# Spectral tower of a token network on one core: the product over channels in four 64x64 matmuls, edge counts by pairs of bins, and the sorting work spread anew

## The chip, the cores and the metric

The kernel runs on one core of a Trainium2 chip. The number that counts is the device time of one execution, in microseconds (us). A core has five engines: TensorE (PE, with its weight loads shown apart as PEld), VectorE (DVE), ScalarE (ACT), GpSimd (POOL) and SyncE (SP), which issues most of the DMAs. Engines wait for each other on semaphores.

## The reference

The reference is a chain of stages on 128 images of 64x64 values (for the later stages 8192 tokens of 64 values). The first stage, a Fourier tower, is what the change touches:

```python
def fourier_layer(x, fw_i):                      # x: batch, 32 channels, 64, 64
    x_ft = jnp.fft.rfft2(x, s=(M, N), norm='ortho')
    lo = jnp.einsum('bixy,ioxy->boxy', x_ft[:, :, :M1, :M2], w_lo)    # M1 = M2 = 12
    hi = jnp.einsum('bixy,ioxy->boxy', x_ft[:, :, -M1:, :M2], w_hi)
    ...
    return jnp.fft.irfft2(out_ft, s=(M, N), norm='ortho')

h = conv1x1(concat([x, grid]), p_w, p_b)         # 3 -> 32 channels
for i in range(4):
    x1 = fourier_layer(h, fw[i])
    x1 = relu(conv1x1(x1, w1_w[i], w1_b[i]))
    x1 = conv1x1(x1, w2_w[i], w2_b[i])
    h = h + x1
h = relu(conv1x1(h, q1_w, q1_b))                 # 32 -> 4 channels: the head
h = conv1x1(h, q2_w, q2_b)                       # 4 -> 1
```

Then come attention and expert layers (named a0, e0, a1, e1, a2, e2, a3), and at the end a graph attention over 262,144 edges and 8192 self loops. The kernel needs the edges sorted by their target node. It sorts them in two passes of a counting sort, and hides that work beside the stages before: DVE ranks, POOL scatters.

## The kernel before, in words

**The tower's loops.** 128 images go in 4 groups of 32. Each group passes 4 layers; a group and a layer are a unit (16 units, `u`). A unit has 4 chunks of 8 images (`ch`), so there are 64 chunks, numbered n = 4u + ch here. Chunk 0 of a unit also holds what the unit does once: `mix` (L568, spectral weights), `turn` (L579) and, in all but the last layer, `blend` (L673) at the end of the unit before. A first layer also has a prologue (L519 to L547).

**A chunk on PE.** `to_x` (L597) transforms along x: 128 matmuls of 96 rows by 32 columns. Then the 32 channels come in 8 steps `s` of 4 channels: `to_y` (L638) transforms two steps at a time into four PSUM banks (banks 0 to 3), ACT applies bias and relu into the buffer `rr` (L752), and `use` (L600) reads it twice. The first reader, L615, is the product over channels: it collects, for the head, what this layer adds to the 4 head channels. It is a 128x128 weight `proj` with 512 columns, once for each half `hf` of the 64 y values, accumulated over the 8 steps in banks 4 and 5. The partitions of `rr` are (4 channels, 32 y), so `proj` is 4x4 numbers, each times a 32x32 identity. The second reader, L624, transforms back along y with 96 columns (8 matmuls per step, full 128x128 weights). The last layer of a group doesn't need it. `from_x` (L659) ends a chunk in the other layers. All this is fp32; PE runs each fp32 matmul as two instructions.

**What ties a chunk to DVE.** After the 8 steps DVE adds banks 4 and 5 to `qa` (L847, two instructions) and signals `q_added`. The first L615 of the next chunk waits for it, since it overwrites bank 4. DVE does its share of the sorting of this chunk before that add (`rank_part(n)`, L832). So a chunk ends when both are through, PE with its steps and DVE with its sorting items and the add.

**The sorting items.** First pass (columns): 128 bins are counted over 2112 keys per partition (`count`, L2600, one bin per instruction), 52 of them by ACT ahead of the tower; PE sums the counts once (L611, L612, before the first L615 of chunk `column_offset_at`, which waits for the counts, and then for DVE's offsets, L2612 to L2616); then 6 parts of the keys (132, 176, 264, 484, 528 and 528 wide) are ranked, one item for each bin: a compare, a running sum, a copy of one column and a predicated copy (L2619, L2622, L2625, L2626). When a part is ranked, POOL scatters it: one indirect DMA for each of the 2112 columns (L2661). Second pass (rows): when POOL is through, SP loads the scattered pairs (L455), DVE makes keys (L2656, L2657), counts 65 bins and ranks 4 parts of 528, 260 items in all. Items that the tower has no room for come in fixed places later: 8 at the tower's end, TOKEN_ITEMS in the stage that loads the tower's output and all weights (`token_stage`, L3377), 16 in a0, 90 in e0.

**What sets the order.** `slot_us(n)` gives each chunk a time budget in us, `spread_items` fills it with items at planned costs (2.5 for a count, 0.4 + 0.0042 x width for a rank), and `column_plan` and `row_plan` hold the item numbers at which each chunk starts. The row pass may begin at chunk ROW_CHUNK = 51. SP loads the scattered pairs when its program comes to that chunk and POOL has signalled `scattered`.

Of the kernel before, what the change touches and what calls it, by code (L numbers as in the profile page):

```python
# [14 lines left out]
P = 128  # L15
NB = 128
S = 64
D = 64
# [93 lines left out]
def fno_constants():  # L112
# [26 lines left out]
    s2 = s2[0:2, :, :, :, :, 0:2].reshape(24, 2, 2 * 64).transpose(1, 0, 2)  # L139
    gap = np.zeros((8, 2 * 64))  # L140
    c["to_y"] = np.concatenate([s2[0], gap, s2[1], gap] * 2, 0)
    c["from_y"] = f1.reshape(P, 2 * 96)
# [19 lines left out]
    c["eye32"] = np.tile(np.eye(32), (4, 1))  # L162
# [8 lines left out]
def fno_layout(x, p_w, p_b, fw, w1_w, w1_b, w2_w, w2_b, q1_w, q1_b, q2_w, q2_b):  # L171
# [26 lines left out]
    b1 = np.zeros((LAYERS, 4, 32, 8), f32)  # L198
    w2r = np.zeros((LAYERS, CH, 8, 4, 32), f32)
    for cg in range(8):  # L200
        for cc in range(4):
            b1[:, cc, :, cg] = w1_b[:, channel(cg, cc), None]
            w2r[:, :, cg, cc] = w2_w[:, :, channel(cg, cc), None]
# [5 lines left out]
    o["q1_rep"] = np.repeat(q1_w.T[:, :, None], 32, 2).reshape(CH, P)  # L209
    o["q1_b_rep"] = np.repeat(q1_b, 32)[:, None]  # L210
    o["q2_rep"] = np.repeat(q2_w[0], 32)[:, None]
# [7 lines left out]
def fno_prelude(t, d, f, ranks):  # L219
# [6 lines left out]
    with ExitStack() as ctx:  # L226
# [6 lines left out]
        proj = sb("proj", [P, LAYERS, 8, 4, 32])  # L233
# [4 lines left out]
        with t.stage("even_in", "odd_in", "small_in", "fold_done", "fold_turned", "s_done", "s_moved", "b_sum", "qb_done", "own", "even_kept", "odd_kept", "proj_kept", "proj_ready", "fold_crossed", "under_counted") as \  # L238
# [51 lines left out]
            def _(v):  # L290
                c = Chain(v, own)
                early = iter(range(ACT_BINS, EARLY_COUNTS))

                def count_some(n):
                    for i in itertools.islice(early, n):
                        ranks.count(v, c, i, COLS)

                count_some(5)
# [3 lines left out]
                c.link(v.tensor_scalar(f.head[:], const["eye32"][:], q2_rep[:, 0:1], None, ALU.mult))  # L302
                count_some(5)
                v.wait_ge(s_done, 1)
                c.link(v.tensor_copy(proj_s[:].rearrange("p l c o -> p (l c o)")[:, 0:32 * LAYERS + 4], t.bank[7][:, 0:32 * LAYERS + 4]))
                eye = const["eye32"][:].unsqueeze(1).broadcast_to([P, 4, 32])
                for l in range(LAYERS):
                    for j in range(8):
                        c.link(v.tensor_tensor(proj[:, l, j], eye, bc(proj_s[:, l, j, :], 32), ALU.mult))
                c.link(v.tensor_tensor(f.proj0[:].rearrange("p (o y) -> p o y", y=32), eye, bc(proj_s[:, LAYERS, 0, :], 32), ALU.mult))  # L310
                v.sem_inc(proj_ready, 1)
                v.wait_ge(qb_done, 1)
                c.link(v.tensor_tensor(f.qb[:], t.bank[6][:, 0:1], q1_b_rep[:], ALU.add))
                for l in range(LAYERS):
# [8 lines left out]
                    if l in (1, 2):  # L323
                        count_some(8 if l == 1 else EARLY_COUNTS - ACT_BINS - 18)

# [21 lines left out]
class Fno:  # L347

    def __init__(self, t, ctx, d):
        sb = lambda name, shape: t.sb("f_" + name, shape, ctx=ctx)  # L350
        self.const = {k: sb(k, d[k].shape) for k in ("to_x", "to_y", "from_y", "from_y1", "from_x", "eye32", "lift", "q2_b_rep")}
# [3 lines left out]
        self.head = sb("head", [P, 32])  # L355
# [3116 lines left out]
```

## Time and profile before

| | us |
|---|---|
| three timed runs | 10031.47, 10034.33, 10067.39 |
| median | 10034.33 |
| span of the profiled execution | 10048.4 |
| TensorE busy in it | 8145.5 (81%) |
| VectorE busy | 7005.4 (70%) |
| ScalarE busy | 4663.9 (46%) |
| GpSimd busy | 5541.9 (55%) |

The profiled execution has no other time than its span of 10048.4 us, which lies between the timed runs. The tower with its preparation takes the first 4033 us of it. The page shows busy shares; for a stretch the table by windows is of more use, since each stage has another limit. Times in a timeline are the start from the span's beginning, then the duration. Matmuls overlap, so the distance between two starts tells more than a duration. "x4" is the number of instructions merged into a row.

### The profile page before, as it was taken

The page shows a single profiled execution, that of the slowest core. Times are in us where ns is not written, and L with a number is a line of the kernel's source. Part 1 is how long each engine was busy: PE and PEld are TensorE (multiplying, and loading weights), DVE is VectorE, ACT ScalarE, POOL GpSimd, SP SyncE. Part 2 cuts the span into 40 slices and gives each one's busy share as a digit, 9 for nine tenths or more (in the row PEclk, how much of TensorE's full clock was granted, in tenths as well). Part 3 has the DMA queues.
Part 4 walks back from the last instruction along what each step waited for, and adds up shares of the span by engine and source line. Part 5 has one row for each costly group of instructions (what it writes and reads, how often), then busy time and mean ns, then how long its engine had stood idle before and what let it go on. Part 6 is the DMA issues. An engine that isn't in the chain of part 4 may idle for free. (4 is left out here: it accounts for less than half of the span.)

```text
span 10048.4 us, 187067 instructions
## 1 busy us (share of the span) xinstructions
PE 8145.5 (81%) x76884; PEld 4885.9 (49%) x76884; DVE 7005.4 (70%) x10524; ACT 4663.9 (46%) x10721; POOL 5541.9 (55%) x5545
## 2 busy tenths in 40 slices
PE   4899899999999998477788888887767688888837
PEld 2666566656666665222222222223332577777732
DVE  7898888740000677678999999995454578888852
ACT  5333444444444434233677877784333333333322
POOL 0077777777777000174566666676243077777740
PEclk7999899989998999588899999997667589999966
DMA  5000100010001000100000000000100022222210
GB/s 182 22 24 25 58 27 25 26 38 23 23 23 37 31 24 4 35 2 1 3 2 2 2 2 2 2 2 1 1 1 1 13 44 45 51 45 45 46 51 9
DMA packets 275177, 251.33 MB, mean 25 GB/s; under 512 B 204433, under 2 KB 258449, under 8 KB 268628
## 3 DMA queue, kind: packets, MB, share of 16 engines
q1 hardware_dynamic: 97012, 219.26, 6.7%
q0 software_dynamic: 177312, 20.11, 3.4%
q8 instruction: 607, 9.95, 0.4%
q14 instruction: 246, 2.02, 0.1%
HBM read 178.16 MB, written 60.82 MB: 24 GB/s over the span
## 5 line engine op out<-in xcount | busy, mean ns | idle before, releaser
L2507 POOL DMA_INDIRECT sorted<-by_row_rows,r_pos x2112 | 2086.7, 988 | 2170.6 <-ACT e_xt L1354 1096.2
L2661 POOL DMA_INDIRECT sorted<-r_rows,r_pos x2112 | 2142.8, 1015 | 1153.2 <-issue 642.7
L2180 DVE TENSOR_TENSOR a_top<-bank,a_k 128x2048 f32<-128x2048 f32 x896 | 1972.5, 2278 | 8.5 <-ACT a_qs L2235 6.9
L2960 PE MATMUL bank<-g_parts,g_hot 128*128 128x256 bf16 x11088 | 1326.2, 286 | 250.0 <-issue 136.1
L2943 POOL DMA_INDIRECT g_g<-table,g_el x1188 | 1169.9, 985 | 362.3 <-issue 362.3
L2960 PEld LDWEIGHTS bank<-g_parts,g_hot 128*128 128x128 bf16 x11088 | 1133.0, 103 | 443.0 <-issue 144.1
L2382 PE MATMUL bank<-a_top,sc_pick_row 128*32 128x512 f32 x7168 | 953.2, 616 | 307.0 <-DVE a_top L2180 291.4
L2622 DVE TENSOR_TENSOR_SCAN r_work<-r_hit,r_base 128x528 f32<-128x528 bf16 (+4 forms) x1028 | 1072.8, 1044 | 33.6
L615 PE MATMUL bank<-f_space,f_proj 128*128 128x512 f32 x2048 | 988.3, 610 | 90.7 <-ACT f_space L752 82.5
L847 DVE TENSOR_TENSOR f_qa<-f_qa,bank 128x512 f32<-128x512 f32 x128 | 82.2, 684 | 1354.5 <-PE bank L624 1141.1
L2228 ACT ACTIVATE a_over<-a_k,a_qs 128x64 f32<-128x64 f32 x4096 | 1021.4, 337 | 0.0
L752 ACT ACTIVATE f_space<-bank,f_b1r 128x512 f32<-128x512 f32 x1024 | 635.2, 686 | 451.9 <-PE bank L638 451.9
L624 PEld LDWEIGHTS bank<-f_from_y,f_space 128*128 128x128 f32 x6144 | 748.5, 192 | 185.1 <-issue 185.1
L624 PE MATMUL bank<-f_from_y,f_space 128*128 128x96 f32 x6144 | 739.3, 274 | 0.0
L615 PEld LDWEIGHTS bank<-f_space,f_proj 128*128 128x128 f32 x2048 | 354.2, 190 | 578.4 <-issue 426.5
L2626 DVE COPY_PREDICATED r_work<-r_hit,r_work 128x528 f32<-128x528 uint16 (+4 forms) x1028 | 613.7, 597 | 0.0
L743 ACT ACTIVATE f_space<-bank 128x384 f32<-128x384 f32 x384 | 188.6, 491 | 900.7 <-PE bank L624 900.7
L2382 PEld LDWEIGHTS bank<-a_top,sc_pick_row 128*32 128x32 f32 x7168 | 151.5, 109 | 878.0 <-DVE a_top L2180 757.4
L1423 DVE TENSOR_TENSOR e_hid<-e_hid,bank 128x512 f32<-128x512 f32 x512 | 345.8, 686 | 310.5 <-ACT e_hid L1382 172.7
L2972 ACT ACTIVATE g_apart<-g_near,sc_place 128x512 f16<-128x512 f16 x462 | 307.7, 713 | 509.5 <-DMA g_near<-near 311.9
L597 PE MATMUL bank<-f_to_x,f_bb 96*32 96x128 f32 x16384 | 499.8, 284 | 31.9 <-ACT f_bb L732 31.9
L638 PE MATMUL bank<-f_space,f_to_y 56*64 56x512 f32 x4096 | 498.5, 602 | 20.4 <-ACT f_space L737 20.4
(587 smaller groups left out, 11825.1 us busy)
## 6 DMA issues: line engine op xcount, KB each, us to landing
f_wm<-folded SPq DMA_DIRECT2D x16, 4608.0 KB
sorted<-r_rows,r_pos POOLq DMA_INDIRECT x2112
sorted<-by_row_rows,r_pos POOLq DMA_INDIRECT x2112, 2.1
g_near<-near SPq DMA_DIRECT2D x231, 128.0 KB
states<-g_st SPq DMA_DIRECT2D x33, 768.0 KB, 4.0
g_g<-table,g_el POOLq DMA_INDIRECT x1188
fp_raw<-t_modes SPq DMA_DIRECT2D x4, 2304.0 KB, 15.4
folded<-fp_turned SPq DMA_DIRECT2D x16, 576.0 KB, 9.3
```

The costliest lines, as they stand in the source:

```text
L615: last = pe.matmul(t.bank[4 + hf][:, :], proj[:, cg].rearrange("p o y -> p (o y)"), rr[:, s % 3 * 2 + hf, :], start=(s == 0), stop=(s == 7))
L624: last = pe.matmul(t.bank[6 + s % 2][:, b * 96:(b + 1) * 96], rr[:, s % 3 * 2 + hf, b * P:(b + 1) * P], const["from_y"][:, hf * 96:(hf + 1 ...
L752: last = act.activation(rr[:, s % 3 * 2 + hf, :], t.bank[s % 2 * 2 + hf][:, :], ACT.Relu, bias=f.b1r[:, u % LAYERS, cg:cg + 1])
L2180: v.tensor_tensor(top[:, n % RD].rearrange("p q (h s) -> p q h s", s=S), q, kk, ALU.max).then_inc(top_done, 1)
L2228: last = act.activation(over[:, slot, q, e, :], ks[:, k % 2, e, :], ACT.Relu, scale=-1.0, bias=qs[:, k % 2, slot, at_q:at_q + 1])
L2382: last = pe.matmul(sums[k % 2][32 * q:32 * q + 32, :], t.pick_row[:, i, :], rhs, start=False, stop=(i == I16 - 1), skip_group_check=True)
L2507: p.indirect_dma_start(out=self.dst, out_offset=bass.IndirectOffsetOnAxis(ap=self.idx[:, k:k + 1], axis=0), in_=self.rows[:, k, :], in_off ...
L2622: c.link(v.tensor_tensor_scan(self.run[:, 0:n], self.hit[:, 0:n], self.hit[:, 0:n], self.base[:, i:i + 1], ALU.add, ALU.bypass))
L2626: c.link(v.copy_predicated(self.posf[:, 0:n], self.hit[:, 0:n].bitcast(mybir.dt.uint16), self.run[:, 0:n]))
L2661: p.indirect_dma_start(out=self.dst, out_offset=bass.IndirectOffsetOnAxis(ap=self.pos[:, at:at + 1], axis=0), in_=self.rows[:, part % 2, a ...
L2943: p.indirect_dma_start(out=g[:, c % GB, j, :], out_offset=None, in_=d["table"], in_offset=bass.IndirectOffsetOnAxis(ap=el[:, at, 0:1], axi ...
L2960: last = pe.matmul(out, hot[:, n % HB, k, j * P:(j + 1) * P], parts[:, k, s].rearrange("p f i -> p (f i)"), start=(k == 0 and s == 0), sto ...
```

## The change

Four things change together.

**1. The product over channels.** y is now split in sixteens: the partitions of `rr` are (2 halves of 16 y, 4 channels, 16 y). The product then doesn't mix the upper and the lower 64 partitions, and each 128x128 matmul becomes two of 64 rows by 64 columns. For the second `hf` the output halves are swapped (`part ^ hf`), so that the four matmuls of a step stand in the four different quadrants of the array.

**2. The transform to y.** To write its output in that order, each 56x64 matmul of `to_y` becomes two of 56x32: 16 matmuls where 8 stood, in 8 different places (2 of 64 rows, 4 of 32 columns).

**3. The counts.** `count_two` counts two bins in one instruction: a key of the upper half of the bins is folded onto the lower half and weighs 4096, others weigh 1; the sum is split into two counts afterwards. 76 column counts become 38 instructions, 65 row counts 33, with three preparing instructions and five splitting ones for each pass.

**4. The plan.** The budgets, the first row chunk, and with them all item numbers change. The preparation holds 26 pair counts where it held 21 counts. The offsets come in chunk 0, not 1. A chunk without a unit's extra work from number 17 to 27 still has 16 ranks; such a chunk of a last layer has 8 where it had 10. The tower now holds 86 row ranks, not 137, and TOKEN_ITEMS, which takes what is left, is 60, not 9.

The core of the diff:

```diff
@@ to_y and use
                     for hf in range(2):
-                        last = pe.matmul(t.bank[4 + hf][:, :], proj[:, cg].rearrange("p o y -> p (o y)"), rr[:, s % 3 * 2 + hf, :], start=(s == 0), stop=(s == 7))
+                        for part in range(2):
+                            rows, to = slice(64 * part, 64 * part + 64), 64 * (part ^ hf)
+                            last = pe.matmul(t.bank[4 + hf][to:to + 64, :], proj[rows, cg].rearrange("p o y -> p (o y)"), rr[rows, s % 3 * 2 + hf, :], start=(s == 0), stop=(s == 7), skip_group_check=True)
...
                                 base = half_of(cg, k)
-                                last = pe.matmul(t.bank[s % 2 * 2 + hf][64 * k:64 * k + 64, :], const["to_y"][base:base + 56, hf * 64:(hf + 1) * 64], aa[base:base + 56, cg, :], start=True, stop=True, skip_group_check=True)
+                                for part in range(2):
+                                    to, col = 64 * part + 32 * k, 64 * hf + 32 * part
+                                    last = pe.matmul(t.bank[s % 2 * 2 + hf][to:to + 32, :], const["to_y"][base:base + 56, col:col + 32], aa[base:base + 56, cg, :], start=True, stop=True, skip_group_check=True)
@@ the counts
-    def count(self, v, c, i, n):
-        c.link(v.tensor_scalar(self.seen[:, 0:n], self.key[:, 0:n], self.t.iota[:, i:i + 1], None, ALU.is_equal, ALU.add, accum_out=self.hist[:, i:i + 1]))
+    def pair_bins(self, v, c, first, pairs):
+        c.link(v.tensor_scalar(self.seen, self.key[:], float(first + pairs), None, ALU.is_ge))
+        c.link(v.tensor_scalar(self.weight, self.seen, SECOND - 1.0, 1.0, ALU.mult, ALU.add))
+        c.link(v.scalar_tensor_tensor(self.low_key, self.seen, -float(pairs), self.key[:], ALU.mult, ALU.add))
+
+    def count_two(self, v, c, first, j):
+        c.link(v.scalar_tensor_tensor(self.seen, self.low_key, float(first + j), self.weight, ALU.is_equal, ALU.mult, accum_out=self.two[:, j:j + 1]))
+
+    def part_bins(self, v, c, first, pairs):
...
@@ the plan
-EARLY_COUNTS = 73
-ROW_CHUNK = 51
+EARLY_PAIRS = 26
+ROW_CHUNK = 54
...
     if ch:
-        return 28 if u % LAYERS == LAYERS - 1 else 44
+        return 23 if u % LAYERS == LAYERS - 1 else 42
     if u % LAYERS == 0:
-        return 131 if u else 143
-    return 53 if u % LAYERS == LAYERS - 1 else 67
+        return 126 if u else 110
+    return 47 if u % LAYERS == LAYERS - 1 else 61
...
-            if done == offset and spent > 18:
+            if done == offset and spent > (40 if n == 0 else 18):
```

The order of instructions on PE, from the last transform of the first unit through its first chunk's first two steps, before. Names are output<-inputs; `f_space` is the buffer that holds `aa` and `rr`, `f_proj` is `proj`, and the sizes are columns of the weight by columns streamed:

```order
L597 MATMUL bank<-f_to_x,f_bb 32x128 x128
L638 MATMUL bank<-f_space,f_to_y 64x512 x8
L615 MATMUL bank<-f_space,f_proj 128x512 x2
L624 MATMUL bank<-f_from_y,f_space 128x96 x8
L638 MATMUL bank<-f_space,f_to_y 64x512 x8
L615 MATMUL bank<-f_space,f_proj 128x512 x2
```

The same place after the change:

```order
L606 MATMUL bank<-f_to_x,f_bb 32x128 x128
L651 MATMUL bank<-f_space,f_to_y 32x512 x16
L620 MATMUL bank<-r_hist,sc_before 128x128
L621 MATMUL bank<-r_hist,sc_ones 128x128
L626 MATMUL bank<-f_space,f_proj 64x512 x4
L635 MATMUL bank<-f_from_y,f_space 128x96 x8
```

The transform to y has twice the matmuls at half the width, the product twice the matmuls at half the width and half the rows, and the two sums over the counts now stand in the first chunk.

DVE, from the end of the preparation to the first rank of the tower, before. `x3` and `x55` are counts of one bin each (`r_work,r_hist<-r_key`), `f_qa` is the add that ends a chunk:

```order
L2600 TENSOR_SCALAR r_work,r_hist<-r_key,sc_iota 128x2112 x3
L321 STREAM_TRANSPOSE fp_turned<-bank 128x64 x72
L64 UNCONDITIONAL_BRANCH
L790 UNCONDITIONAL_BRANCH
L2600 TENSOR_SCALAR r_work,r_hist<-r_key,sc_iota 128x2112 x55
L2607 SCALAR_TENSOR_TENSOR r_hist<-r_under 128x52
L2608 TENSOR_TENSOR r_hist<-r_hist,r_under 128x52
L847 TENSOR_TENSOR f_qa<-f_qa,bank 128x512 x2
L2612 SCALAR_TENSOR_TENSOR r_base<-bank,r_hist 128x128
L2615 TENSOR_TENSOR r_base<-r_base,bank 128x128
L2616 TENSOR_TENSOR r_base<-r_base,bank 128x128
L2619 TENSOR_SCALAR r_hit<-r_key,sc_iota 128x132
```

DVE at the same place after the change, without the five rows that split the sums:

```order
L2630 SCALAR_TENSOR_TENSOR r_work,r_base<-r_pos 128x2112 x7
L330 STREAM_TRANSPOSE fp_turned<-bank 128x64 x72
L64 UNCONDITIONAL_BRANCH
L803 UNCONDITIONAL_BRANCH
L2630 SCALAR_TENSOR_TENSOR r_work,r_base<-r_pos 128x2112 x12
```

```order
L2645 SCALAR_TENSOR_TENSOR r_hist<-r_under 128x52
L2646 TENSOR_TENSOR r_hist<-r_hist,r_under 128x52
L2650 SCALAR_TENSOR_TENSOR r_base<-bank,r_hist 128x128
L2653 TENSOR_TENSOR r_base<-r_base,bank 128x128
L2654 TENSOR_TENSOR r_base<-r_base,bank 128x128
L2657 TENSOR_SCALAR r_hit<-r_key,sc_iota 128x132
```

The offsets now stand ahead of the first add of the tower, with 76 ranks between them and that add, where 55 counts stood ahead of it.

## Rows read from the trace of the kernel before

**Rows 1.** The page: busy us, share of the span, instructions of PE.

```profile
PE 8145.5 (81%) x76884; PEld 4885.9 (49%) x76884; DVE 7005.4 (70%) x10524; ACT 4663.9 (46%) x10721; POOL 5541.9 (55%) x5545
```

**Rows 2.** Windows: stretch, length, busy by engine, PE clock, DMA share, GB/s.

```profile
326.40:389.40 63.00, 60.43 (x702) 44.22 (x696) 45.93 (x162) 24.41 (x45) 0.00 (x0) 0.97 0.01 2
389.40:447.00 57.60, 50.62 (x544) 35.03 (x536) 52.76 (x188) 22.61 (x41) 0.00 (x0) 0.99 0.01 2
504.00:1161.00 657.00, 600.77 (x7984) 405.78 (x7984) 576.86 (x1381) 272.75 (x504) 510.22 (x448) 0.97 0.10 32
1161.00:3490.70 2329.70, 2144.03 (x27416) 1503.10 (x27420) 979.75 (x1491) 963.93 (x1783) 1629.57 (x1662) 0.95 0.10 30
1352.40:1402.90 50.50, 49.15 (x536) 34.74 (x532) 41.08 (x68) 20.11 (x37) 38.57 (x39) 1.00 0.03 2
2302.80:2353.30 50.50, 49.15 (x540) 34.74 (x534) 1.31 (x3) 20.10 (x37) 38.31 (x41) 1.00 0.03 2
3024.80:3056.40 31.60, 28.20 (x309) 12.94 (x300) 1.28 (x2) 14.23 (x24) 24.02 (x25) 1.00 0.37 96
3490.70:4004.80 514.10, 474.03 (x6152) 315.78 (x6140) 399.21 (x621) 215.67 (x396) 0.00 (x0) 0.97 0.04 13
4033.00:4062.00 29.00, 0.00 (x0) 0.00 (x0) 22.31 (x36) 0.00 (x0) 0.00 (x0) 0.50 0.62 199
```

**Rows 3.** Timeline of PE within chunk 34: start, duration, operation, idle before.

```profile
2323.15 1.98 PE L615 MATMUL bank<-f_space,f_proj 128*128 128x512 f32 x4
2324.97 1.92 PE L624 MATMUL bank<-f_from_y,f_space 128*128 128x96 f32 x16
2326.73 1.91 PE L615 MATMUL bank<-f_space,f_proj 128*128 128x512 f32 x4
2328.47 1.92 PE L624 MATMUL bank<-f_from_y,f_space 128*128 128x96 f32 x16
2330.32 1.95 PE L638 MATMUL bank<-f_space,f_to_y 56*64 56x512 f32 x16
2332.20 0.70 PE L615 MATMUL bank<-f_space,f_proj 128*128 128x512 f32 x1
```

**Rows 4.** Timelines of PE and ACT at the start of chunk 47, last layer.

```profile
3031.55 1.95 PE L638 MATMUL bank<-f_space,f_to_y 56*64 56x512 f32 x16 [0.73 <-ACT f_space L737]
3034.85 1.98 PE L615 MATMUL bank<-f_space,f_proj 128*128 128x512 f32 x4 [1.35 <-ACT f_space L752]
...
3033.53 2.42 ACT L752 ACTIVATE f_space<-bank,f_b1r 128x512 f32<-128x512 f32 x4 [2.04 <-PE bank L638]
```

**Rows 5.** Groups of PE, 257.1 to 258.95 us: mixing of modes.

```profile
L568 PE MATMUL bank<-f_wm,f_spec 64*32 64x64 f32 x128 | 1.8, 221 | 1.6 <-issue 1.6
```

**Rows 6.** Counts, first product and offsets: by line, then timeline.

```profile
L2600 DVE TENSOR_SCALAR_CACHE_REDUCE r_work<-r_key,sc_iota x55: 2411/2412/2415, 189.3 to 321.9; 128x2112 bf16<-128x2112 bf16 x55
...
L615 PEld LDWEIGHTS bank<-f_space,f_proj x2048: 186/190/337, 287.9 to 4002.4; 128*128 128x128 f32 x187
...
339.15 0.42 DVE L2612 TENSOR_TENSOR_SCAN r_base<-bank,r_hist 128x128 f32<-128x128 f32 x1 [12.78 <-PE bank L612]
```

**Rows 7.** Groups of DVE in chunk 2, 389.4 to 447 us.

```profile
L2622 DVE TENSOR_TENSOR_SCAN r_work<-r_hit,r_base 128x132 f32<-128x132 bf16 x46 | 22.7, 493 | 1.6
```

**Rows 8.** POOL's scatter by line: ns, starts, idle; then SP's reload.

```profile
L2661 POOL DMA_INDIRECT sorted<-r_rows,r_pos x2112: 955/962/1912, 500.1 to 3295.6; - x192
...
  DVEq L810: 510.5, 2
...
3298.96 6.45 SPq L455 DMA_DIRECT2D r_rows<-sorted  x4
```

**Rows 9.** Timeline of DVE at the token stage's end and a0's start.

```profile
4051.74 1.32 DVE L2622 TENSOR_TENSOR_SCAN r_work<-r_hit,r_base 128x528 f32<-128x528 bf16 x1
...
4054.33 1.32 DVE L2622 TENSOR_TENSOR_SCAN r_work<-r_hit,r_base 128x528 f32<-128x528 bf16 x1
...
4062.14 0.69 DVE L953 TENSOR_REDUCE a_mean<-h 128x8 f32<-128x512 f32 x1 [5.65 <-PEq L72]
```

More of the change, by code:

```diff
@@ L161, in fno_constants @@
     c["grid_spectrum"] = sp.reshape(16, KYG * KX * 2 * GI)
-    c["eye32"] = np.tile(np.eye(32), (4, 1))
+    c["eye16"] = np.tile(np.eye(16), (8, 1))
+    lift_to, head_from = np.zeros((4, 32, 2, 2, 16)), np.zeros((2, 4, 16, 2, 32))
+    for hf in range(2):
+        for place in range(2):
+            for y in range(16):
+                lift_to[:, 16 * (place ^ hf) + y, hf, place, y] = 1.0
+                head_from[place, :, y, hf, 16 * (place ^ hf) + y] = 1.0
+    c["lift_to"], c["head_from"] = lift_to.reshape(P, 64), head_from.reshape(P, 64)
     return {k: np.ascontiguousarray(v.astype(np.float32)) for k, v in c.items()}
@@ L291, in _ @@
                 c = Chain(v, own)
-                early = iter(range(ACT_BINS, EARLY_COUNTS))
+                early = iter(range(EARLY_PAIRS))
                 def count_some(n):
-                    for i in itertools.islice(early, n):
-                        ranks.count(v, c, i, COLS)
-                count_some(5)
+                    for j in itertools.islice(early, n):
+                        ranks.count_two(v, c, ACT_BINS, j)
+                ranks.pair_bins(v, c, ACT_BINS, COLUMN_PAIRS)
+                count_some(4)
                 v.wait_ge(small_in, 16 * (len(small) + 5))
@@ L526, in prologue @@
                             pe.wait_ge(q0_moved, gi * 8)
[L527 removed]
+                        pe.matmul(t.bank[6 + n % 2][:, :], f.proj0[:, n // 4 * P:n // 4 * P + P], feat[:, n * 512:(n + 1) * 512], start=True, stop=True).then_inc(q0_done, 1)
                     pe.wait_ge(x0_moved, gi + 1)
@@ L680, in head @@
                             for hf in range(2):
-                                last = pe.matmul(t.bank[n][:, b * D + hf * 32:b * D + hf * 32 + 32], qa[:, hf, (8 * n + b) * P:(8 * n + b + 1) * P], f.head[:], start=True, stop=True)
+                                last = pe.matmul(t.bank[n][:, b * D + hf * 32:b * D + hf * 32 + 32], qa[:, hf, (8 * n + b) * P:(8 * n + b + 1) * P], f.head[:, hf * 32:hf * 32 + 32], start=True, stop=True)
                         last.then_inc(o_done, 1)
@@ L2589, in __init__ @@
         self.run, self.posf = work[:, 0, :], work[:, 1, :]
-        self.seen = work[:].rearrange("p a c -> p (a c)").bitcast(BF16)
+        self.seen = work[:].rearrange("p a c -> p (a c)").bitcast(BF16)[:, 0:COLS]
         self.hist = sb("hist", [P, P])
```

88 lines of the change are left out of this document (53 added, 35 removed).

## The prediction

> **What bounds the kernel now.** I read the page first: PE is busy 81% of the span [rows 1], more than any other engine, but that is a mean over stages, so the table by windows comes next [rows 2]. It shows three kinds of chunk in the tower. Chunk 34, with no sorting beside it, takes 50.5 us, of which PE is busy 49.15; chunk 18, with 16 ranks on DVE (41.08 us busy), takes the same 50.5. So an ordinary chunk (layers 0 to 2) is PE's. Chunk 47, of a last layer, takes 31.6 with PE busy 28.2. Chunks 1 and 2 take 63.0 and 57.6 us: there DVE's sorting sets the pace (46 ranks of 132 columns in chunk 2 [rows 7], DVE busy 52.76 of 57.6). The token stage, 29 us, has nothing on PE at all: DMAs (0.62 of their time) and 9 ranks on DVE. The timeline of PE then says what a chunk is made of [rows 3, 4], and the line of POOL what runs in parallel with the whole tower: the scatter from 500.1 to 3295.6 us, with the reload of its result at 3298.96, just as the row pass begins [rows 8].
>
> **The product.** A step's L615 is 4 instructions from 2326.73 to 2328.47 us, 1.74 us, 0.43 each [rows 3]. After the change 8 narrower ones stand in 4 quadrants. That quadrants run side by side is in the trace: L638 before is 16 instructions of 56x64 with 512 columns, and the next block starts 1.88 us after it, so four took 0.43 us together, as one L615 takes alone. So the product becomes 0.86 us.
>
> **The switches.** L624 takes 1.76 us ahead of L615 (2324.97 to 2326.73) but 1.85 ahead of L638; L638 takes 1.88 where four times 0.43 is 1.72; the L615 after it 1.82 instead of 1.74 [rows 3]. Going into quadrants and back out costs 0.09 + 0.16 + 0.08, about 0.34 us a pair (0.14 in, 0.2 out), from full array to full array nothing. After the change each step pays it. For the 4 steps between two L624: 1.74 becomes 0.86 + 0.34, saving 0.53. For the 4 right after a transform to y, which paid 0.2 for leaving quadrants already: 1.94 becomes 1.2, saving 0.72. Sum 4 x 0.53 + 4 x 0.72 = 5.0 us, so an ordinary chunk goes from 50.5 to 45.5. Bounds: switches between tile shapes free gives 6.9 us, twice their price gives 3.
>
> **The transform to y.** Not seen before: 64 rows by 32 columns with 512 columns streamed. Nearest is L568, 64x32 with 64 columns: 128 in 1.8 us, their starts within 1.57 us, 12.2 ns each [rows 5]. At L638's pace of 0.43 us for 512 columns, 64 columns take 54 ns, so 4.4 ran at once, above the four that every other line reaches. If eight run at once the block stays at 1.72 us; with four it becomes 3.44. I take no change, since these instructions are eight times as long, and what holds L568 at 12.2 ns can be the rate of issue; the other end is +1.72 us four times a chunk.
>
> **The last layers.** There ACT comes in. The transform starts at 3031.55, relus of its two steps at 3033.53 for 2.42 us, the product at 3034.85 [rows 4]. The next transform overwrites the banks, so it waits for both relus: 1.98 + 2.42 + 0.1 = 4.5 us a pair of steps at least. Before PE needed 5.5 (1.88 + two products + switch), so this did not bind. Four pairs, with 0.9 for the last product and 8.1 ahead of the first transform, make 27.1 us instead of 31.6: 4.5 saved, not 6.9.
>
> **DVE beside it.** 16 ranks at 2.59 us [rows 9] and the adds (1.3) make 42.9 us, under 45.5; a last-layer chunk has 8 ranks, 22.3, under 27.1. A pair count isn't in the trace; its nearest row is the single count, 2.41 us plus a read [rows 6], 2.46. I take 2.46, since both stream 2112 keys; between half and 1.1 times that the answer is the same, as in chunk 55 16 of them (39 us) lie under 45.5.
>
> **The tower's start.** The preparation gets 7 pair counts instead of 3 counts ahead of its last transposes: between 0 and 10 us later, I take 4. PE's first product, at 287.9 us [rows 6], thus comes at 292. The offsets now wait for it (2 us), and 76 ranks of 132 columns at 1.22 us (57.6 us less adds for 46 [rows 2, 7]) stand before the first add: chunk 0 ends at 388, not 326. PE waits some 50 us in chunk 1. Then, with 1.37 us for a rank of 176 columns (between 1.22 and 2.59 by width): chunk 1 has 44 ranks, to 444; chunk 2 8 + 30, to 497; chunk 3 36, to 548, where it was 504. Chunks 4 to 15: two with a unit's extra work at 85.6, six ordinary ones of which three are still DVE's (49, 47, 47), the last layer's 72 + 3 x 27.1. That is 604 us against 657 [rows 2]: chunk 15 ends at 1152, 9 us earlier than before.
>
> **The middle and the end.** Chunks 16 to 53 took 2329.7 us: 30 of them save 5.0, 8 save 4.5, together 186, so chunk 54 starts at 3296. Chunks 54 to 63 took 514.1 and save 6 x 5.0 + 4 x 4.5 = 48; the wait for the row offsets, now in an ordinary chunk with 13 ranks, takes back 3.5. The tower ends 9 + 186 + 48 - 3.5 = 239 us earlier.
>
> **POOL.** Its first part is ranked 8 ranks into chunk 2, at 455 instead of 500.1. It took 2796 us, 11 of them waiting after the first wait (510.5 less 499.7); later parts now wait for DVE about 16, 3 and 9 us. End: 455 + 2796 + 17 = 3268, reload by 3272. Chunk 54 starts at 3296, so nothing waits, with 24 us of cover; chunk 53 would have waited.
>
> **The token stage.** 51 more ranks at 2.59 (4051.74 to 4054.33 [rows 9]) are 132 us. Nothing covers them: the 29 us stage is already DVE's to its end but for 5.65 us of barrier. What the later stages do stays where it was.
>
> **Sum.** -239 + 132 = -107 us on the profiled span of 10048.4, which is 14 above the median and inside the timed runs; on the median of 10034.3 that makes 9927.
>
> **A rule against the change.** L638 before has two row groups writing one PSUM bank (k = 0 and 1 of a step) and still runs four at once [rows 3]. The Trainium skill, page "TensorEngine Tiling (Array Packing)", Restrictions and Gotchas (PSUM Pressure), says that different row tiles cannot access the same bank at the same time. By that rule the two halves of each product, which share bank 4 or 5, would run one after the other, and the trace disagrees with it, so it keeps only a small chance. The same page's Tiling Modes lists eight tiles of 64x32; no row shows eight at once.
>
> **The rivals.**
> - *Four streams, not eight.* What speaks for it: most lines stop at four, and L568 only just passes. The transform costs 6.9 us more in each ordinary chunk, so it goes to 52.4, +1.9; a last-layer chunk to 34, +2.3. Chunks 5 to 15 are then no longer DVE's but PE's: chunk 15 ends at 1228, +67; then 36 x 1.9 + 12 x 2.3 + 3.5 = 100; with the 132 of the token stage +300: 10334. It decides as soon as a block of 32 transforms takes over about 2.9 us. Chance 0.13.
> - *Halves one after the other.* A product stays at 1.72 us and pays the switches, again +1.9 in an ordinary chunk; last-layer chunks, and with them the sum, come out nearly as above: about 10300. Against it: the four at once in L638. Chance 0.03.
> - *Switches between tile shapes free.* An ordinary chunk at 43.6, hardly above DVE's 42.9. The tower then runs into POOL: chunk 54 would start at 3226, its keys wait until 3272, it ends at 3303 instead of 3342, and six more chunks save 1.9: -52 to 9877. Chance 0.14.
> - *Switches twice as dear*, or PE's clock granted low more often (it is 1.00 within chunks, 0.95 over the middle [rows 2]): +1.9 in 36 chunks, 9995. Chance 0.14.
> - The forecast itself, 9885 to 9980: 0.53. Something not seen, slower than 10090 with nothing above: 0.03.
>
> **How the numbers follow.** What a measurement of this kernel can tell from no change is about 0.5%, 50 us: 9984 to 10084. Faster: 0.53 + 0.14 + a fifth of the fourth = 0.70. Same: the rest of the fourth, 0.11. Slower: 0.19. The range runs from 9850 (free switches and a little more) to 10030 (dear switches and a preparation 10 us longer), which leaves out the two serial cases and the unseen, 0.19.
>
> **What would show it.** L626 (the product) with 8 instructions and L635 starting 1.0 to 1.1 us after it; L651, 32 instructions with the next block 1.9 us later (3.5 if four streams); chunk 34 at 45.5 us by windows; a last-layer chunk at 27; DVE's first L864 near 387; POOL's first row near 455, its last near 3267, and SP's reload before chunk 54; a token stage of 161 us. Wrong would be the whole sum if the block of transforms grows, and the size of it if switches or ACT's turn are mis-sized.

## The result and the profile after

| | us |
|---|---|
| before, four timed runs | 10031.47 to 10067.39, median 10044.83 |
| changed kernel, four timed runs | 9905.14 to 9931.88, median 9913.49 |
| ratio | 0.9866, 95% interval 0.9852 to 0.9881 |
| span of the profiled execution | 9910.4 (before 10048.4) |

The page of the changed kernel, answering to [rows 1]: busy us, share of the span, instructions.

```profile
PE 7804.4 (79%) x83028; PEld 4612.5 (47%) x83028; DVE 6834.7 (69%) x10375; ACT 4660.9 (47%) x10721; POOL 5520.2 (56%) x5545
```

PE has 6144 more instructions and is busy 341 us less. The table by windows, changed kernel, answering to [rows 2]; its stretches are chunk 0 from 292 us on (PE's first product starts at 287.6), chunk 1, chunks 4 to 15, 16 to 53, chunk 18 (with ranks), 34 (without), 47 (last layer), 54 to 63, and the token stage. A chunk ends with DVE's second add (L864).

```profile
292.00:382.00 90.00, 44.39 (x606) 29.72 (x605) 82.36 (x294) 20.08 (x36) 0.00 (x0) 0.73 0.00 1
382.00:437.10 55.10, 46.07 (x624) 31.58 (x624) 50.47 (x179) 20.07 (x36) 0.00 (x0) 0.90 0.01 2
540.40:1141.30 600.90, 538.70 (x9136) 353.22 (x9136) 526.18 (x1173) 272.53 (x504) 464.72 (x407) 0.96 0.11 34
1141.30:3290.80 2149.50, 1956.30 (x31060) 1346.15 (x31064) 822.35 (x1330) 963.00 (x1783) 1600.24 (x1638) 0.94 0.10 31
1324.20:1369.70 45.50, 44.14 (x630) 30.42 (x624) 41.01 (x67) 19.99 (x37) 34.83 (x36) 1.00 0.03 3
2195.80:2241.40 45.60, 44.24 (x636) 30.52 (x628) 1.29 (x3) 20.08 (x37) 34.62 (x37) 1.00 0.03 3
2855.80:2882.80 27.00, 22.24 (x404) 8.77 (x394) 1.28 (x2) 14.18 (x25) 20.60 (x22) 1.00 0.47 112
3290.80:3758.80 468.00, 421.50 (x7116) 271.86 (x7104) 326.79 (x473) 215.51 (x396) 0.00 (x0) 0.97 0.05 16
3785.10:3942.00 156.90, 0.00 (x0) 0.00 (x0) 149.27 (x241) 0.00 (x0) 0.00 (x0) 0.50 0.12 37
```

The tower ends at 3758.8 us instead of 4004.8, so 246 us earlier; the token stage takes 156.9 us instead of 28.9, so 128 of the 246 are lost again there. Chunks 54 to 63 took 514.1 and take 468.0; the middle took 2329.7 and takes 2149.5.

The timeline of PE within chunk 34 (start, duration, operation), answering to [rows 3]:

```profile
2213.54 1.95 PE L651 MATMUL bank<-f_space,f_to_y 56*32 56x512 f32 x32
2215.42 1.09 PE L626 MATMUL bank<-f_space,f_proj 64*64 64x512 f32 x8
2216.44 2.02 PE L635 MATMUL bank<-f_from_y,f_space 128*128 128x96 f32 x16
2218.39 1.09 PE L626 MATMUL bank<-f_space,f_proj 64*64 64x512 f32 x8
```

Read the distances between starts. The product now holds PE for 1.02 us (2215.42 to 2216.44) instead of 1.74. The 32 transforms to y hold it 1.88 us, exactly as long as the 16 before. The block behind a product, L635, has not changed at all and yet takes 1.95 us, where it took 1.76 ahead of a product and 1.85 ahead of a transform: PE now changes the shape of its tiles more often, and each change costs something (see the grouped order below).

PE and ACT at the start of chunk 47, a last layer, answering to [rows 4]:

```profile
2862.46 1.95 PE L651 MATMUL bank<-f_space,f_to_y 56*32 56x512 f32 x32 [0.73 <-ACT f_space L750]
2865.77 1.09 PE L626 MATMUL bank<-f_space,f_proj 64*64 64x512 f32 x8 [1.36 <-ACT f_space L765]
2866.92 1.95 PE L651 MATMUL bank<-f_space,f_to_y 56*32 56x512 f32 x32
```

From one transform to the next it is 4.46 us. ACT's relus of the pair:

```profile
2864.45 2.42 ACT L765 ACTIVATE f_space<-bank,f_b1r 128x512 f32<-128x512 f32 x4 [2.04 <-PE bank L651]
```

They end at 2866.87, and the next transform follows 0.05 us later: the last layers are ACT's now.

Answering to [rows 6]: the pair count (durations min, median, max), and DVE's timeline at the first offsets.

```profile
L2630 DVE SCALAR_TENSOR_TENSOR r_work<-r_pos x71: 2312/2357/2360, 46.6 to 3416.0; 128x2112 bf16<-128x2112 bf16 x71
```

```profile
286.44 0.42 DVE L2650 TENSOR_TENSOR_SCAN r_base<-bank,r_hist 128x128 f32<-128x128 f32 x1 [67.77 <-PE bank L621]
...
287.65 0.26 DVE L2657 TENSOR_SCALAR r_hit<-r_key,sc_iota 128x132 bf16<-128x132 bf16 x1
...
288.88 0.26 DVE L2657 TENSOR_SCALAR r_hit<-r_key,sc_iota 128x132 bf16<-128x132 bf16 x1
```

A pair of bins costs 2.36 us and a short read, as much as one bin did. A rank of 132 columns is 1.23 us here (287.65 to 288.88), and 76 of them stand before the add of chunk 0, which comes at 380.7.

POOL's scatter, answering to [rows 8], and SP's reload:

```profile
L2699 POOL DMA_INDIRECT sorted<-r_rows,r_pos x2112: 954/959/1914, 447.3 to 3239.6; - x192
...
  DVEq L824: 459.6, 2
```

```profile
3241.89 51.19 SPq L464 DMA_DIRECT2D r_rows<-sorted  x4
```

POOL starts its last scatter 51 us before chunk 54 starts, at 3290.8. The row of the reload spans its four DMAs, the last of which starts at 3292.8. In the token stage (answering to [rows 9]) DVE ranks without a gap until a barrier, and then comes a0's first row:

```profile
3942.00 0.69 DVE L970 TENSOR_REDUCE a_mean<-h 128x8 f32<-128x512 f32 x1 [1.22 <-PEq L72]
```

### The profile page after: what moved, and what is told of

It reads as the page before. It is cut to its first block and busy times, and to the rows that moved or that the text cites. A ratio compares the mean times of both kernels' runs of the same rounds, so it can differ in the third digit from the quotient of the medians.

```text
span 9910.4 us, 199204 instructions
## 1 busy us (share of the span) xinstructions
PE 7804.4 (79%) x83028; PEld 4612.5 (47%) x83028; DVE 6834.7 (69%) x10375; ACT 4660.9 (47%) x10721; POOL 5520.2 (56%) x5545
## 5 line engine op out<-in xcount | busy, mean ns | idle before, releaser
L864 DVE TENSOR_TENSOR f_qa<-f_qa,bank 128x512 f32<-128x512 f32 x128 | 82.2, 683 | 1364.9 <-PE bank L635 1157.0
L635 PEld LDWEIGHTS bank<-f_from_y,f_space 128*128 128x128 f32 x6144 | 719.6, 193 | 314.9 <-issue 159.1
L765 ACT ACTIVATE f_space<-bank,f_b1r 128x512 f32<-128x512 f32 x1024 | 634.5, 686 | 411.3 <-PE bank L651 411.3
L635 PE MATMUL bank<-f_from_y,f_space 128*128 128x96 f32 x6144 | 782.7, 281 | 0.0
L626 PE MATMUL bank<-f_space,f_proj 64*64 64x512 f32 x4096 | 561.4, 618 | 161.2 <-ACT f_space L765 95.5
L651 PE MATMUL bank<-f_space,f_to_y 56*32 56x512 f32 x8192 | 502.1, 599 | 23.7 <-ACT f_space L750 20.5
L606 PEld LDWEIGHTS bank<-f_to_x,f_bb 96*32 96x32 f32 x16384 | 449.9, 114 | 85.8 <-ACT f_bb L745 34.5
```

Source lines behind the costliest of these rows:

```text
L606: last = pe.matmul(out, bb[0:96, at:at + wide], const["to_x"][:, r * P:(r + 1) * P], start=True, stop=True, skip_group_check=True)
L635: last = pe.matmul(t.bank[6 + s % 2][:, b * 96:(b + 1) * 96], rr[:, s % 3 * 2 + hf, b * P:(b + 1) * P], const["from_y"][:, hf * 96:(hf + 1 ...
L765: last = act.activation(rr[:, s % 3 * 2 + hf, :], t.bank[s % 2 * 2 + hf][:, :], ACT.Relu, bias=f.b1r[:, u % LAYERS, cg:cg + 1])
```

## The experiments

Times are medians with their lowest and highest run, ratios are to the kernel before, run beside each, with their 95% interval. Starts, ends and windows are those of the one execution that was profiled. Line numbers shift from kernel to kernel; the names of the tiles and the shapes stay.

**One half of the change each.** The first kernel has the matmul part alone, with the counts, slots and ROW_CHUNK of before.

```diff
+                        for part in range(2):
+                            rows, to = slice(64 * part, 64 * part + 64), 64 * (part ^ hf)
+                            last = pe.matmul(t.bank[4 + hf][to:to + 64, :], proj[rows, cg]...
...
 ROW_CHUNK = 51
```

> The kernel before with only the matmul part of the change (product in 64x64 tiles, transform to y in 32-column tiles); counts one by one, the plan and ROW_CHUNK 51 as before. My theory: the matmuls get faster as in the changed kernel (45.6 us a chunk from about chunk 9 on), but without the rest of the change most of that gain ends at POOL. Chunk 51 then starts near 3110 us, POOL still ends its scatter near 3295, so chunk 51's keys wait and it ends near 3333 (before 3351.7); chunks 52 to 63 save about 47 more, the tower ends near 3939 (before 4004.8), the token stage stays at 29 us, the span is 66 us shorter: about 9978, ratio 0.9934. The rival that the two halves of the change are independent says that the tower ends some 240 us earlier and the time is about 9800.

Measured: 9970.03 us (9962.33 to 9974.03), ratio 0.9911 (0.9888 to 0.9934). Chunks 34 and 51 by windows, then DVE's timeline in chunk 51:

```profile
2190.90:2236.50 45.60, 44.24 (x632) 30.52 (x628) 1.28 (x2) 20.09 (x37) 34.49 (x36) 1.00 0.03 3
3110.50:3321.00 210.50, 48.51 (x632) 34.56 (x620) 26.57 (x29) 21.56 (x40) 131.89 (x138) 0.63 0.05 13
```

```profile
3289.21 0.43 DVE L2668 TENSOR_SCALAR r_work<-r_rows 128x528 int32<-128x528 int32 x1 [178.69 <-DMA r_rows<-sorted]
```

An ordinary chunk takes 45.6 us, as in the changed kernel, so that gain is the matmuls' alone. Chunk 51 takes 210.5 us, for DVE waits 179 us for keys that POOL (last scatter at 3283.2) hasn't delivered, and PE waits behind DVE's add. The tower ends at 3920.7, 84 us earlier than before. Less the 165 us lost in this chunk that is 3756, where the changed kernel's tower ends (3758.8). By this estimate the matmuls carry the whole gain of the tower, and the place of the row pass decides whether it arrives; no kernel was run with the matmul part and only ROW_CHUNK moved.

The second kernel has the sorting part alone:

```diff
-EARLY_COUNTS = 73
-ROW_CHUNK = 51
+COLUMN_PAIRS = (P - ACT_BINS) // 2
+EARLY_PAIRS = 26
+ROW_CHUNK = 54
...
-        return 28 if u % LAYERS == LAYERS - 1 else 44
+        return 23 if u % LAYERS == LAYERS - 1 else 42
```

> The kernel before with only the sorting part of the change (counts by pairs, slots, ROW_CHUNK 54, 60 ranks in the token stage); the matmuls as before. My theory: it is slower. Chunk 0 ends near 382, chunk 15 near 1195 (before 1161), ordinary chunks are 50.5 us, last-layer ones 31.6; POOL ends near 3240 with nobody waiting for it; the tower ends near 4037 (before 4004.8), and the token stage is 157 instead of 29 us: about 10200, ratio 1.016. The rival, that pair counts save DVE time on the path, says that the tower ends earlier than before and the time is at most 10130.

Measured: 10224.88 us (10196.73 to 10233.77), ratio 1.0161 (1.0134 to 1.0188). The tower ends at 4033.7, chunks take 50.5 us as before; the token stage by windows:

```profile
4059.00:4216.90 157.90, 0.00 (x0) 0.00 (x0) 149.29 (x242) 0.00 (x0) 0.00 (x0) 0.50 0.11 37
```

Its span is 173 us longer: 129 in the token stage, 29 at the tower's end (PE waits behind the 76 ranks in chunk 0, which ends at 391.2 instead of 326.4; by chunk 15 39 us of that are left, by chunk 63 29), and 18 from a0's start on, in stages that the change doesn't touch (more on these below), less 3 between tower and token stage. Cheaper counts lie beside PE and earn nothing there. The expectation had chunk 0 at 382 and POOL's end near 3240; they came at 391 and 3262. Tower ends: -84 and +29 alone, -246 together. The halves don't add up, since each moves what the other waits for: the faster matmuls need the later row pass, and the later row pass puts 51 ranks into the token stage whether or not PE is faster.

**Two quadrants instead of four.** The tables `lift_to` and `head_from` are laid out to match the other place of the output; no other edit.

```diff
-                            rows, to = slice(64 * part, 64 * part + 64), 64 * (part ^ hf)
+                            rows, to = slice(64 * part, 64 * part + 64), 64 * part
```

> The changed kernel, but both halves hf of the product go to the same two quadrants (output rows 64*part instead of 64*(part^hf), with the tables for the lift and the head to match), so that only two different tiles are in use. My theory (four quadrants run at once, each tile serves one matmul at a time): the product block goes from 1.02 to 1.88 us, an ordinary chunk from 45.6 to 52.4, a last-layer chunk from 27.0 to about 31.9, and the time is about 10287, slower than before (ratio 1.024). The rival that the halves ran one after the other already, or that two tiles suffice, says no change against the changed kernel (9913).

Measured: 10284.48 us (10273.26 to 10294.15), ratio 1.0225 (1.02 to 1.0249). PE within chunk 34 of this kernel:

```profile
2403.39 1.94 PE L626 MATMUL bank<-f_space,f_proj 64*64 64x512 f32 x8
2405.26 2.03 PE L635 MATMUL bank<-f_from_y,f_space 128*128 128x96 f32 x16
```

The same 8 instructions, of the same shape, take 1.87 us where they took 1.02, and chunk 34 takes 52.4 us, as expected: four 64x64 matmuls run at once only if they lie in four different quadrants, and what decides is the `^ hf`. This also settles the rule weighed in the prediction. In the changed kernel the two halves of a product write one bank from two row groups; by the Trainium skill, page "TensorEngine Tiling (Array Packing)", Restrictions and Gotchas, they would take turns, and the block would have been the 1.87 us seen here. It is 1.02, so the trace disagrees with the rule for row groups that write different partitions of the bank.

**The transforms alone.** The kernel before, with the transform to y cut in 32 pieces:

```diff
-    last = pe.matmul(t.bank[...][64 * k:64 * k + 64, :], const["to_y"][base:base + 56, hf * 64:(hf + 1) * 64], ...
+    for part in range(2):
+        to, col = 64 * k + 32 * part, 64 * hf + 32 * part
+        last = pe.matmul(t.bank[...][to:to + 32, :], const["to_y"][base:base + 56, col:col + 32], ...
```

> The kernel before with only the transform to y cut into 32 instead of 16 matmuls (32 output columns each, eight tiles in use instead of four); product and plan as before. My theory (eight tiles run at once): the block from it to the next one stays at 1.88 us, the chunk at 50.5, the time that of before (ratio 1.00). The rival of four streams: the block takes 3.6 us, a chunk 57.4, the time about 10400.

Measured: 10039.23 us (10020.3 to 10060.32), ratio 0.9994 (0.998 to 1.0009). PE within chunk 34 of this kernel:

```profile
2318.04 1.95 PE L640 MATMUL bank<-f_space,f_to_y 56*32 56x512 f32 x32
2319.92 1.98 PE L615 MATMUL bank<-f_space,f_proj 128*128 128x512 f32 x4
```

Eight at once: 32 instructions of 512 columns in 1.88 us, as long as 16 of the double width took. The rival of four streams, the dearest of the prediction, is out.

**The price of a switch.** In layers 0 to 2 two transforms from y are put one behind the other, T P T P F F P T P F F P T P F F P P F F instead of T P F T P F P F T P F P F T P F P F P F (T to y, P product, F from y). Blocks of one kind that touch count once, so 14 changes of kind are left of 19. ACT's copies (`spread`) follow the new order, which the cut of the diff doesn't show.

```diff
-                        use(u, ch, 2 * pair - 1)
-                        use(u, ch, 2 * pair)
+                        product(u, ch, 2 * pair - 1)
+                        from_y(u, ch, 2 * pair - 2)
+                        from_y(u, ch, 2 * pair - 1)
+                        product(u, ch, 2 * pair)
```

> The changed kernel with the order of PE's blocks changed in layers 0 to 2: the transforms from y of two steps stand one after the other (P2 T P3 F2 F3 P4 T P5 F4 F5 ...), so that PE goes from small tiles to the full array and back 4 times in a chunk instead of 8; ACT's copies follow. If the price (0.34 us a pair) is paid between small tiles and the full array only: an ordinary chunk goes from 45.6 to about 44.5, the time from 9913 to about 9873. If every change of tile shape costs its 0.16 to 0.2 us, also that between the transform to y (56x32) and the product (64x64): 45.1 and about 9893. If the extra 0.34 us isn't a matter of shapes at all: 45.9 and about 9925 (T1 starts 0.3 us later).

Measured: 9903.34 us (9885.33 to 9908.99), ratio 0.9846 (0.9827 to 0.9866); the kernel before took 10061.17 beside it, so on the 10044.83 of the first comparison that is 9890, 23 less than the changed kernel. The intervals of the two ratios overlap, so the gain rests on the windows and not on these times. Its chunk 34 by windows, then PE within it:

```profile
2184.00:2228.90 44.90, 43.47 (x635) 30.31 (x628) 1.28 (x2) 20.07 (x37) 34.23 (x36) 1.00 0.03 3
```

```profile
2202.84 3.81 PE L638 MATMUL bank<-f_from_y,f_space 128*128 128x96 f32 x32
2206.58 1.09 PE L626 MATMUL bank<-f_space,f_proj 64*64 64x512 f32 x8
2207.60 1.95 PE L654 MATMUL bank<-f_space,f_to_y 56*32 56x512 f32 x32
2209.48 1.09 PE L626 MATMUL bank<-f_space,f_proj 64*64 64x512 f32 x8
...
2221.89 1.95 PE L626 MATMUL bank<-f_space,f_proj 64*64 64x512 f32 x16
2223.77 3.81 PE L638 MATMUL bank<-f_from_y,f_space 128*128 128x96 f32 x32
```

Two F together take 3.74 us, which is 1.95 + 1.79: the second has next to no surcharge. Two P together take 1.88, which is 1.02 + 0.86. But a P ahead of a T takes 1.02 (2206.58 to 2207.60), though both are small tiles, and a T ahead of a P 1.88. So the first theory, that only the way between quadrants and the full array is paid, falls, and the second holds: each change of the tile's shape is paid. The rows above merge a block's instructions; from start to start of the single ones, where the steady pace is broken only beside a change, T to P costs 0.19 us, P to F 0.19, F to P 0.14, F to T 0.12 and P to T 0.14. The new order has four P to F, three F to T and one F to P less and three P to T more: 0.83 us. The second transform starts 0.14 later behind the first product (1.16 instead of 1.02), which leaves 0.69; 0.7 was measured. The Trainium skill says so too, "TensorEngine Tiling (Array Packing)", Tiling Modes: changing the tiling mode, and not just the tile, drains the engine. The trace agrees, with 0.12 to 0.19 us a change.

**A plan that uses the cover.** Chunk 53 starts at 3245.2 in the changed kernel, behind POOL's last scatter. In chunk 56 DVE was busy 29.7 of 84.3 us, because the offsets may come only within the first 18 planned us of a chunk; they were put off to chunk 57, where DVE waited for PE's sums:

```profile
3482.56 0.29 DVE L2650 TENSOR_TENSOR_SCAN r_base<-bank,r_hist 128x65 f32<-128x65 f32 x1 [15.46 <-PE bank L621]
```

```diff
-ROW_CHUNK = 54
+ROW_CHUNK = 53
-        return 23 if u % LAYERS == LAYERS - 1 else 42
+        return 24 if u % LAYERS == LAYERS - 1 else 42
+    if n > ROW_CHUNK:
+        return 55 if u % LAYERS == LAYERS - 1 else 67
-    costs = [5.0] * ROW_PARTS + ...
+    costs = [2.8] * ROW_PARTS + ...
```

> The changed kernel with another plan of the row pass: ROW_CHUNK 53 (it starts at 3245.2 us in the changed kernel, POOL's scatter ends at 3239.6), keys planned at 2.8 instead of 5.0 us so that the offsets come in an ordinary chunk right behind the last pair count (chunk 55) and chunk 56 is filled, 9 instead of 8 ranks in last-layer chunks; 17 instead of 60 ranks are left for the token stage. My theory (a rank in the token stage costs its 2.59 us, in the tower nothing as long as DVE stays under PE, and POOL's cover of 50 us at chunk 54 is idle): the tower ends as in the changed kernel, near 3759, the token stage takes 157 - 43 x 2.59 = 46 us, the time is about 9802 (ratio 0.976). The rival, that the cover is needed (chunk 53's keys wait) or that DVE then sets the pace of chunks 53 to 63: the tower ends 20 to 60 us later, 9820 to 9860.

Measured: 9808.49 us (9797.67 to 9831.83), ratio 0.9774 (0.9748 to 0.9801). By windows, chunks 53 and 55:

```profile
3248.80:3294.50 45.70, 44.34 (x640) 30.62 (x632) 36.90 (x39) 20.21 (x37) 0.00 (x0) 1.00 0.08 26
3340.10:3390.50 50.40, 47.31 (x589) 32.12 (x580) 34.69 (x53) 19.74 (x36) 0.00 (x0) 0.93 0.02 3
```

Chunk 53 is no longer than any other, with its 16 sorting items. The tower ends at 3762.7, 4 us later than in the changed kernel, of which 3.6 were there when chunk 53 began (3248.8 against 3245.2). a0 starts at 3834.3 instead of 3942.0, so 107.7 us earlier: 43 ranks at 2.59 are 111, less those 4. The edit moves the start of the row pass, fills chunk 56 and adds a rank to last-layer chunks; what each is worth was not tried.

**Both together.** The new plan with the grouped order (no other edit).

> The new plan and the grouped order of PE's blocks together. The tower is 0.7 us faster in each ordinary chunk, so chunk 53 would start near 3222, but POOL ends its scatter near 3243: chunk 53's keys wait about 20 us, and about 10 us of the grouped order's gain stays. My theory (POOL bounds this one): about 9795. If POOL didn't matter: about 9770.

Measured: 9789.4 us (9782.5 to 9802.37), ratio 0.975 (0.9727 to 0.9774). Its chunk 53 by windows, and DVE's wait in it:

```profile
3219.30:3291.90 72.60, 56.87 (x917) 41.41 (x908) 36.91 (x38) 28.76 (x52) 19.16 (x20) 0.93 0.11 32
```

```profile
3249.46 0.43 DVE L2705 TENSOR_SCALAR r_work<-r_rows 128x528 int32<-128x528 int32 x1 [30.17 <-DMA r_rows<-sorted]
```

The chunk comes 29.5 us earlier than in the new plan and ends 2.6 us earlier: POOL is the bound again. The tower ends at 3750.0, 12.7 us earlier, where the expectation had 10. A faster tower now needs an earlier end of POOL's scatter (some 2792 us from first to last), so an earlier start.

**Sums earlier.** The row at 286.44 above says more than when the ranks start: DVE had stood idle for 67.8 us. The counts were ready at 218.7, and what it waited for are two matmuls (L620, L621) that PE has in its program right before chunk 0's first product. The two are moved into the preparation, with the wait for the counts ahead of them and PE's wait for DVE's offsets behind them (not shown):

```diff
 def prologue(gi):
     ...
+    if gi == 0:
+        pe.wait_ge(counted, 1)
+        pe.matmul(t.bank[4][:, 0:P], t.before[:, :], ranks.hist[:, 0:P], start=True, stop=True)
+        pe.matmul(t.bank[5][:, 0:P], t.ones[:, :], ranks.hist[:, 0:P], start=True, stop=True).then_inc(summed, 1)
     for b in range(PAIRS):
```

> The changed kernel with one thing moved: PE sums the first counts (L620, L621) in the preparation of group 0, behind the product of the features, instead of right before chunk 0's first product. In the changed kernel the counts are ready at 218.7 us and DVE then stands idle for 67.8 us until PE comes to the sums. My theory (the 76 ranks that start at 287.7 make chunk 0 late): the ranks start near 220 and are through near 313, chunk 0 ends near 317 instead of 382, chunks 1 to 3 stay DVE's (55, 53, 51 us), POOL starts near 382 and ends near 3174, the tower ends near 3693 and the time is about 9848 (ratio 0.980). The rival that PE's or the preparation's own work sets the end of chunk 0, or that the sums delay the preparation: less than 20 us gained.

Measured: 9863.82 us (9850.7 to 9880.71), ratio 0.983 (0.9809 to 0.985). DVE's timeline, then chunk 0 behind it by windows, then POOL:

```profile
219.15 0.42 DVE L2656 TENSOR_TENSOR_SCAN r_base<-bank,r_hist 128x128 f32<-128x128 f32 x1 [0.92 <-PE bank L541]
```

```profile
221.00:317.90 96.90, 85.49 (x1587) 62.94 (x1588) 85.79 (x306) 48.20 (x97) 0.00 (x0) 0.89 0.13 51
```

```profile
L2705 POOL DMA_INDIRECT sorted<-r_rows,r_pos x2112: 952/959/1917, 383.3 to 3172.1; - x192
```

Chunk 0 ends at 317.9 instead of 382.0, where 317 was expected, the tower at 3696.3 instead of 3758.8. The wait was the cause of the slow start, and ending it costs 0.34 us of PE's waiting. By the medians only 50 us arrive, and the time is 16 above the expected 9848; from a0's start on this execution took 5981 us, 13 more than the changed kernel's.

**All three.** Early sums, grouped order and new plan, with 9 more ranks in chunk 0.

> Early sums, grouped order and new plan together, and the slot of chunk 0 raised from 110 to 119 (9 more ranks there). My theory: against the grouped order with the new plan (9789) the start gives about 62 us, and since POOL starts some 70 us earlier, chunk 53 (starting near 3157) waits about 18 us for POOL's end near 3172 instead of 30, which gives some 12 more: about 9715 (ratio 0.967). If POOL's end did not move with its start: about 9780.

Measured: 9745.52 us (9729.05 to 9764.36), ratio 0.9716 (0.9693 to 0.9739), the fastest kernel here. The expected 9715 was 30 too low. Chunk 53 by windows:

```profile
3161.50:3228.40 66.90, 56.87 (x917) 41.39 (x908) 36.94 (x38) 28.77 (x52) 14.67 (x16) 0.97 0.11 34
```

POOL ends at 3179.8, not 3172, so the chunk takes 66.9 us, 22 more than an ordinary one; the tower ends at 3686.3, 63.7 us before that of the grouped order with the new plan, where 74 were expected. POOL started earlier than with the early sums alone (378.8 against 383.3) but its own instructions were busy 2146 us instead of 2135; over the eleven profiled executions this varies from 2132 to 2146 with the same 2112 instructions, and the cause is open. The other 20 us lie between this execution (9730) and the median of the four.

## Why the prediction was right

The forecast was 107 us less than before; it became 131 by the medians, 138 by the spans. The mechanisms were the forecast ones. Of the 31 us that the spans gained beyond the forecast 13 are there at a0's start, and some 18 lie behind it, which I take for chance.

- *The product and the switches.* 1.72 became 0.86 us, and the switches cost what they were priced at: an ordinary chunk takes 45.6 where 45.5 was predicted, chunk 34 and chunk 18 alike. From start to start of single instructions F to P costs 0.14 us and P to F 0.19 (0.14 and 0.2 were put on them). Over a round of T P F P F the sum had the old way into T (0.14) and 0.34 for each of two steps, 0.82 in all; the five changes measure 0.82. What the prediction had not seen is that T to P, between two small tiles of different shape, is paid like the others (0.19).
- *The transform to y.* No change, as taken; shown by the trace and by the transforms alone.
- *The last layers.* 27.1 predicted, 27.0 measured, with ACT's relus as the last to come (1.36 us of PE's waiting behind L765). PE alone would need 1.88 us for the transform with its switch and 2 x 0.86 + 0.16 for the two products with theirs, 3.76 a pair of steps; ACT makes it 4.46.
- *DVE beside PE.* In chunk 18 DVE, with its 16 ranks, came to the add 2.8 us before PE did, so PE set the pace, as forecast (42.9 against 45.5). The pair count took 2.40 us from start to start, taken at 2.46.
- *The start.* Chunk 0 ended at 382.0, not 388: the preparation got no longer (first L626 at 287.6, as before at 287.9, where I had added 4), and the offsets stood in front of the product without the 2 us. What followed then was 55.1, 52.6 and 50.7 us, where I had 56, 53 and 51. Chunk 15 ended at 1141.3 instead of 1152: 7.6 of the 10.7 us are there by the end of chunk 3, the rest lies in chunks 4 to 15, 600.9 against 604. The prediction counted the late start as a cost of the plan; it had not seen that two moved matmuls give it back.
- *The middle and the end.* 2149.5 + 468.0 us, where 2143.7 + 469.6 was predicted. The tower: -246 against -239. The start was 10.7 us better than forecast, the middle 5.8 worse and the end 1.6 better, so part of this closeness is luck.
- *POOL.* This step was mis-sized. I had the end at 3268, it was 3239.6: the start came 8 us earlier, and DVE's lateness for the later parts cost 12 us (459.6 less 447.3) instead of 28, and the scatter itself took some 5 less. From it I had concluded that chunk 53 would wait. It would not, and the new plan shows it. That did not touch the total, since chunk 54 was clear of POOL's end either way. The direction of the argument (the row pass must start behind POOL) is what the matmul part alone shows: 179 us of waiting in chunk 51.
- *The token stage.* 51 ranks at 2.59 us are 132; measured 128, as the barrier's idle fell from 5.65 to 1.22 us.
- *Slips in the sums.* From their own terms 0.53 and 0.72 should read 0.54 and 0.74 (1.74 less 1.2, 1.94 less 1.2), 27.1 is 27.0, 42.9 and 22.3 are 42.7 and 22.0, and 9927 less 52 is 9875, not 9877. Together they move the forecast by some 4 us.
- *What is left.* At a0's start the changed kernel is 120.1 us ahead (4062.1 against 3942.0), forecast 107. The other 18 us of the 138 lie behind it, in stages that the change doesn't touch. 17 of them come in the expert stage e1, by windows of before and of the changed kernel:

```profile
6899.20:7202.30 303.10, 212.50 (x839) 93.38 (x840) 112.78 (x201) 90.91 (x155) 134.76 (x136) 0.66 0.03 1
```

```profile
6774.80:7060.90 286.10, 191.98 (x839) 88.45 (x840) 112.19 (x201) 90.73 (x155) 134.97 (x135) 0.73 0.03 1
```

The work is the same and the granted clock is not. I take that for chance and not for the change: from a0's start to the end the eleven profiled executions took 5986 us (before), 5968 (changed), 5994 (matmul part), 6004 (sorting part), 5981 (two quadrants), 5974 (grouped), 5965 (new plan), 5968 (both), 5960 (transforms alone), 5981 (early sums) and 5970 (all three), with the same instructions in all. Within e1, from the first row that writes `e_hid` to the last, it is 189 us before and 171 in the changed kernel, but also 165 in the transforms alone, whose tower ends where that of before does, and 204 in the sorting part. That is one execution of each kernel; why the clock differs between them stays open.

## What to carry to other kernels

When work is hidden beside other work, price each part of a change together with what it uncovers: here the faster matmuls alone gave 84 of the tower's 246 us, because a chunk can't be pulled ahead of the time at which another engine delivers its input, and the new sorting plan alone made the kernel slower, because it put ranks where nothing covers them. After a change that moves one engine, recompute the cover (POOL's end against the chunk that needs it) and fill what has come free; that was worth some 100 us more. Look for an engine that idles long ahead of a few tiny instructions of another: two of them moved forward gave some 50 us by the medians, 62 at the tower's end. Put small matmuls into different quadrants, and count the changes of tile shape, not the instructions.

## What the hardware showed that I had not expected

- Every change of the tile's shape holds PE up, for 0.12 to 0.19 us, also from 56x32 to 64x64 and back. Blocks of one shape in a row cost nothing extra: two products with other weights take 1.88 us for 16 instructions, and two transforms from y, into two banks, 3.74 for 32.
- Eight 64x32 tiles with 512 columns each run at once at no loss (1.88 us for 32). With L568's 64 columns [rows 5] it had looked like 4.4 at once; that line's pace is thus not set by how many such tiles can run at once.
- A wait of PE of about a microsecond can be followed by a spell at the lower clock, or not. In the new plan PE waited 1.36 and 1.15 us around the sums of chunk 55; what stood behind ran at half speed for some 6 us, a granted clock of 0.65 in 9.5 us, so 2.4 and 1.2 GHz mixed:

```profile
3356.55 1.99 PE L626 MATMUL bank<-f_space,f_proj 64*64 64x512 f32 x8 [1.15 <-DVEq L843]
3358.46 3.73 PE L635 MATMUL bank<-f_from_y,f_space 128*128 128x96 f32 x16
```

In the changed kernel the same two waits stand in chunk 57, and the blocks behind them keep full speed:

```profile
3483.67 1.09 PE L626 MATMUL bank<-f_space,f_proj 64*64 64x512 f32 x8 [1.15 <-DVEq L843]
3484.69 2.02 PE L635 MATMUL bank<-f_from_y,f_space 128*128 128x96 f32 x16
```

Of the 5 us by which chunk 55 of the new plan is longer (50.4 instead of 45.6) 3 are this spell, and the rest is the sums with their wait, which both kernels have. What tells the two cases apart was not tried.
